# Folding a router into the attention's output projection, with the normalisation applied after the routing choice

## What is computed

```python
x = _layernorm(x + _L1_attn_ref(...))      # ctx (2048 wide: 16 heads x 128) @ w_dense (2048 x 256)
# _L1_ffn_ref, x is 2048 tokens x 256, 8 experts, top 2, capacity 64
logits = x @ router_w.T
probs = softmax(logits); top_p, top_i = top_k(probs, 2)
# first 64 tokens per expert keep their place: buf = rows gathered by (expert, position)
h = gelu(buf @ w1.T + b1) @ w2.T + b2      # then scattered back, times top_p
x = _layernorm(x + out)
```

## Time and profile before

| | |
|---|---|
| median of 3 runs | 897.33 us (894.57 to 899.10) |
| profiled execution | 895.45 us, of which the span of the trace is 893.7 us |
| PE busy | 824.1 us (92% of the span) |
| DVE busy | 693.6 us (78%) |
| ACT busy | 496.5 us (56%) |
| POOL busy | 390.7 us (44%) |
| layer 0 | 0 to about 390 us |
| layer 1's attention, 64 units | about 390 to 816 us |
| last logits and routing | 816 to 830 us |
| gather, expert network, way back | 830 to 894 us |

### The profile page before, as it was taken

One profiled execution on the slowest core, in us unless ns is written; L12 is line 12 of the kernel. 1 busy time (PEld: TensorE's weight loads), 2 busy tenths in 40 slices (PEclk: granted clock), 3 DMA queues, 4 the chain that ended last, 5 costly groups with the idle time before them and its releaser, 6 DMA issues.

```text
span 893.7 us, 22047 instructions
## 1 busy us (share of the span) xinstructions
PE 824.1 (92%) x8209; PEld 512.8 (57%) x8209; DVE 693.6 (78%) x1921; ACT 496.5 (56%) x1181; POOL 390.7 (44%) x731
## 2 busy tenths in 40 slices
PE   6899999997798998979999999999999999997894
PEld 3455555554454544445556766666767766685374
DVE  5777777777688887678999888888888888866535
ACT  3577777765544534456666555656555565532243
POOL 4556576641365664523333333333333333333454
PEclk8999999999899999999999999999999999998998
DMA  5344432420000000016677656556555655550502
GB/s 180 101 120 108 98 73 85 121 32 8 2 1 1 1 1 1 1 30 120 123 117 123 96 104 104 95 103 101 94 100 104 104 104 96 98 91 1 95 1 95
DMA packets 219034, 67.70 MB, mean 76 GB/s; under 512 B 211360, under 2 KB 214704, under 8 KB 218928
## 3 DMA queue, kind: packets, MB, share of 16 engines
q1 hardware_dynamic: 218928, 66.29, 37.8%
HBM read 17.92 MB, written 4.19 MB: 25 GB/s over the span
## 4 chain that ended last, share of the span: by engine, by line
PE 70%; DVE 14%; issue 5%; DMA 4%; ACT 3%; POOL 3%; SPq 1%; POOLq 0%; DVEq 0%; ACTq 0%
PE bank L467 14%; PE bank L469 14%; PE bank L468 14%; PE bank L594 4%; DMA att<-w_lo 4%; PE bank L825 4%; PE bank L827 3%; PE bank L826 3%; DVE nm L1434 3%; PE bank L541 2%; PE bank L536 2%; PE bank L517 2%; DVE w_lo L1458 2%; PE bank L578 1%; DVE scr L1609 1%
## 5 line engine op out<-in xcount | busy, mean ns | idle before, releaser
L1152 ACT ACTIVATE att<-att,nm 128x512 f32<-128x512 f32 (+3 forms) x256 | 141.4, 553 | 104.5 <-DVE nm L1447 103.1
L1057 ACT ACTIVATE scr<-bank 128x512 bf16<-128x512 f32 (+3 forms) x210 | 111.5, 550 | 88.0 <-PE bank L827 46.1
L467 PE MATMUL bank<-w_hi,scr 128*128 128x256 bf16 (+1 forms) x480 | 145.7, 304 | 2.7 <-DVE scr L1376 1.6
L468 PE MATMUL bank<-w_lo,scr 128*128 128x256 bf16 (+1 forms) x480 | 145.4, 303 | 0.0
L469 PE MATMUL bank<-w_hi,scr 128*128 128x256 bf16 (+1 forms) x480 | 145.3, 303 | 0.0
L1434 DVE TENSOR_REDUCE nm<-bank 128x1 f32<-128x512 f32 (+3 forms) x256 | 110.4, 483 | 39.7 <-PE bank L541 39.6
L2065 POOL TENSOR_SCALAR wqkv_hi<-att,rr 128x512 bf16<-128x512 f32 (+3 forms) x128 | 66.1, 536 | 138.7 <-DVE rr L1464 138.7
L1447 DVE CUSTOM_DVE_ANT_0 att<-bank,consts 128x512 f32<-128x512 f32 (+3 forms) x256 | 113.1, 482 | 15.0 <-PE bank L469 15.0
L1103 ACT ACTIVATE att<-bank 128x512 f32<-128x512 f32 (+1 forms) x192 | 90.7, 528 | 50.1 <-PE bank L578 49.7
L1376 DVE TENSOR_TENSOR scr<-bank,scr 128x256 bf16<-128x256 f32 (+1 forms) x146 | 77.3, 539 | 52.5 <-ACT scr L1057 52.1
L2065 POOL TENSOR_SCALAR w_hi<-att,rr 128x512 bf16<-128x512 f32 (+3 forms) x128 | 66.1, 535 | 105.5 <-DVE rr L1464 105.5
(11 more groups left out here) (242 smaller groups left out, 2038.1 us busy)
## 6 DMA issues: line engine op xcount, KB each, us to landing
scr<-wall_in SPq DMA_DIRECT2D x19, 512.0 KB, 4.7
v_by_token<-scr SPq DMA_DIRECT2D x16, 128.0 KB, 1.8
scr<-v_by_token SPq DMA_DIRECT2D x16, 128.0 KB, 3.3
x_tok<-x_tok_in SPq DMA_DIRECT2D x4, 512.0 KB, 5.1
scr<-x_t_in SPq DMA_DIRECT2D x3, 512.0 KB, 5.5
out<-x_tok SPq DMA_DIRECT2D x3, 512.0 KB, 2.6
scr<-wqkv_in SPq DMA_DIRECT2D x2, 384.0 KB, 3.7
att<-w_hi SPq DMA_TRANSPOSE x32, 3.4
```

The lines of the kernel that those rows point to most:

```text
L467: pe.matmul(out, l_hi, r_hi, start=start, stop=False, skip_group_check=check)
L468: pe.matmul(out, l_hi, r_lo, start=False, stop=False, skip_group_check=check)
L1057: return act.activation(out, in_, ACT.Copy)
L1152: last = act.activation(at, at, ACT.Exp, bias=nm[:, j % 2, qt:qt + 1], scale=-1.0, accum_out=rs[:, j % 2, qt:qt + 1])
```

## The change

- The router matrix of layer 1 is centred on the chip (a sum over features by PE, a subtraction by DVE), and multiplied into the 16 heads' blocks of `w_dense`. For that the 16 blocks, high and low, are turned by 32 more DMA transposes (2 blocks of 128x128 each) that SP issues behind `l1_turns(u)`, three in each of u = 1 to 10 and two in u = 11. PE multiplies them in u = 12 to 15 (`fold_router`, 24 matmuls of 8 columns per unit).
- The product is kept as eight more columns beside each head's 256 in `w_hi` and `w_lo`, so that each projection matmul is 264 columns wide. The residual's share of the logits is added by six matmuls of 8 columns per tile. The logits of y thus stand in the same bank as the attention's output.
- `last_turn`, `last_high`, `last_low` and `last_logits` are gone for all 16 tiles.
- Choices are made on logits without r. The exponentials of all tiles come once, in the tail behind the norms of tiles 12 to 15, and are used for the gates alone.
- In the tail, DVE copies the four tiles' logits as each projection ends, then routes. PE adds the residual of tiles 12 to 15 in PSUM with a matmul by the identity (`add_rows`, f32, 256 columns each). DVE takes their statistics between the first `choose` instructions, POOL makes four deviations at once, ACT norms from PSUM. `gather` takes tiles 0 to 11 for both k first, then 12 to 15. The first of two `keep_busy` goes; the iota matmuls come earlier.

The diff, cut:

```diff
+DW = E + NX
+FOLD_FROM, FOLD_LOADS = 12, 32
             for u in range(NH):
                 l1_turns(u)
+                for hd in range(HEADS):
+                    for part, w in enumerate((w_hi, w_lo)):
+                        if (2 * hd + part) // 3 + 1 == u:
+                            sp.dma_start_transpose(wd_t[part][:, KE * hd:KE * (hd + 1), :],
+                                                   w[:, ds(WD + hd * DW, E)]).then_inc(ld_fold, 16)
...
+            def router_mean():
+                pe.wait_ge(eb_ready, 1)
+                for i, part in enumerate((rw_hi, rw_lo)):
+                    for k in range(KE):
+                        last = pe.matmul(bank[7][:, 0:NX], ones_b[:, :], part[:, 1, k * NX:(k + 1) * NX],
+                                         start=(i == 0 and k == 0), stop=(i == 1 and k == KE - 1))
+                last.then_inc(e["mean"], 1)
+
+            def fold_router(heads):
+                pe.wait_ge(e["router"], 1)
+                pe.wait_ge(ld_fold, 16 * FOLD_LOADS)
+                for hd in heads:
+                    for k in range(KE):
+                        ks = slice(k * NX, (k + 1) * NX)
+                        last = mm3(bank[7][:, hd * NX:(hd + 1) * NX], wd_t[0][:, hd * KE + k, :], wd_t[1][:, hd * KE + k, :],
+                                   router_hi[:, ks], router_lo[:, ks], k == 0, k == KE - 1, True)
...
-                    ws = slice(WD + hd * E, WD + (hd + 1) * E)
-                    last = mm3(out, ct_hi[:, cs], ct_lo[:, cs], w_hi[:, ws], w_lo[:, ws], hd == 0, hd == HEADS - 1)
+                    ws = slice(WD + hd * DW, WD + (hd + 1) * DW)
+                    last = mm3(out, ct_hi[:, cs], ct_lo[:, cs], w_hi[:, ws], w_lo[:, ws], hd == 0, hd == HEADS - 1, True)
+                    if hd == 0:
+                        for k in range(KE):
+                            xs, ks = ds((g - TT) * P, P), slice(k * NX, (k + 1) * NX)
+                            mm3(out[:, E:DW], xt_hi[:, k, xs], xt_lo[:, k, xs], router_hi[:, ks], router_lo[:, ks],
+                                False, False, True)
...
+            def add_rows(t):
+                pe.matmul(bank[DENSE_BANKS[t % TT]][:, 0:E], ident_f, x_tok[:, t * E:(t + 1) * E], start=False, stop=True,
+                          skip_group_check=True).then_inc(e["sum"], 1)
...
-                    if g > TT and j == 2:
-                        hold(pe, c["kvl"], 2 * min(g + 1, NT - 1) + 2)
-                        last_turn(g - TT - 1)
-                    if g > TT and j == 3:
-                        last_logits(g - TT - 1)
+                    if u == TT:
+                        router_mean()
+                    if FOLD_FROM <= u < 4 * TT:
+                        first = 4 * (u - FOLD_FROM)
+                        fold_router(range(first, first + 4))
...
             pe.wait_ge(c["max"], 3 * NH)
+            iota_rows()
...
-            last_turn(DONE)
-            last_turn(DONE + 1)
-            last_logits(DONE)
...
-            pe.wait_ge(e["lgc"], DONE + 1)
-            keep_busy(FILL)
+            pe.wait_ge(e["lgc"], NT)
+            for t in range(DONE, NT):
+                add_rows(t)
             ranks()
             keep_busy(FILL)
             for k in range(KE):
-                for t in range(NT):
+                for t in range(DONE):
+                    gather(k, t)
+            for k in range(KE):
+                for t in range(DONE, NT):
                     gather(k, t)
...
             act.wait_ge(e["cnt"], 1)
             copy(count_b, bank[5][:, 0:2 * P]).then_inc(e["cntb"], 1)
+            act.wait_ge(c["rstd"], DONE + 1)
+            for t in range(DONE, NT):
+                act.activation(x_tok[:, t * E:(t + 1) * E], bank[DENSE_BANKS[t % TT]][:, 0:E], ACT.Identity,
+                               bias=shift_t[:, t:t + 1], scale=rstd_x[:, t:t + 1]).then_inc(e["xn"], 1)
+            act.wait_ge(e["xn"], TT)
+            copy(row_hi[:, DONE * E:NT * E], x_tok[:, DONE * E:NT * E]).then_inc(e["rhi"], 1)
+            act.wait_ge(e["scaled"], 1)
+            act.activation(powers, scaled, ACT.Exp).then_inc(e["ex"], 1)
...
+            for t in range(DONE, NT):
+                dve.wait_ge(c["o"], t + 1)
+                dve.tensor_copy(lg[:, t, :], bank[DENSE_BANKS[t % TT]][:, E:DW]).then_inc(e["lgc"], 1)
+            dve.wait_ge(e["lgc"], NT)
             route_tiles(DONE, NT, 2)
...
-            for t in range(2 * TT):
+            for t in range(DONE):
+                choose(t)
+                if t in (3, 4, 5, 6):
+                    deviation(DONE + t - 3)
+            for t in range(DONE, NT):
                 choose(t)
             rows = slice(DONE * E, NT * E)
             dve.wait_ge(e["rhi"], NB)
             low(row_lo[:, rows], x_tok[:, rows], row_hi[:, rows]).then_inc(e["rlo"], 1)
-            for t in range(2 * TT, NT):
-                choose(t)
```

More of the change, by code:

```diff
@@ L207, in build, with dense_rows, chunk_at, staged @@
         iota8 = consts[:, 768:768 + P]
+        def dense_rows(w):
+            return w[:, WD:WD + HEADS * DW].rearrange("p (h c) -> p h c", c=DW)
+        def chunk_at(w, n):
+            if n in DENSE_CHUNKS:
+                first = 4 * (n - DENSE_CHUNKS[0])
+                return dense_rows(w)[:, first:first + 4, 0:E]
+            return w[:, ds(n * CH + (HEADS * NX if n > DENSE_CHUNKS[-1] else 0), CH)]
+        def staged(n):
+            part = stage[:, ds((n % 2) * CH, CH)]
+            return part.rearrange("p (h c) -> p h c", c=E) if n in DENSE_CHUNKS else part
+        spare = past[:, :, :].rearrange("p i c -> p (i c)").bitcast(F32)
+        router_f, rstd_x = spare[:, 0:KE * NX], spare[:, 32:32 + NT]
+        router_hi, router_lo = [spare[:, 16 + 8 * i:24 + 8 * i].bitcast(BF16) for i in range(2)]
+        wd_t = [scr[:, 4096 + 2048 * i:6144 + 2048 * i].bitcast(BF16).rearrange("p (b q) -> p b q", q=P) for i in range(2)]
         qt_hi = [w_hi[:, TOK * i:TOK * (i + 1)] for i in range(2)]
@@ L334, in build @@
         e = {n: sem(f"ffn_{n}") for n in (
-            "tp", "thi", "tlo", "lg", "lgc", "lgd", "ex", "picks", "rank", "gates", "h", "ge", "hhi", "hlo",
+            "lgc", "ex", "mean", "router", "fold", "fhi", "folded", "sum", "xn", "scaled", "picks", "rank", "gates", "h", "ge", "hhi", "hlo",
             "y", "yr", "bg", "xb", "seq", "agg", "rstd", "x", "dve", "iota", "iotad", "rhi", "rlo", "pick",
@@ L828, in l1_pv @@
                 last.then_inc(c["pv"], 1)
+            def router_mean():
[13 more added lines that the diff above has]
+                                   router_hi[:, ks], router_lo[:, ks], k == 0, k == KE - 1, True)
+                if heads[-1] == HEADS - 1:
+                    last.then_inc(e["fold"], 1)
             def dense_heads(out, g, heads):
@@ L1702, in l1_norm, with center_router, folded_low @@
                 rows = x_tok[:, ds(t * E, E)]
-                i = max(0, t - DONE)
                 hold(dve, c["rstd"], t + 1)
-                dve.tensor_scalar(rows, rows, mv[:, i, 0:1], rstd[:, i:i + 1], ALU.subtract, ALU.mult
+                dve.tensor_scalar(rows, rows, mv[:, 0, 0:1], rstd_x[:, t:t + 1], ALU.subtract, ALU.mult
                                   ).then_inc(c["x"], 1)
+            def center_router():
+                dve.wait_ge(e["mean"], 1)
+                chain = Chain(dve, e["dve"], 0)
+                for k in range(KE):
+                    ks = slice(k * NX, (k + 1) * NX)
+                    chain(dve.scalar_tensor_tensor(router_f[:, ks], bank[7][:, 0:NX], -1.0 / E, rw_f[:, 1, ks],
+                                                   ALU.mult, ALU.add))
+                chain(dve.tensor_copy(router_hi[:, :], router_f[:, :]))
+                dve.tensor_tensor(router_lo[:, :], router_f[:, :], router_hi[:, :], ALU.subtract).then_inc(e["router"], 1)
+            def folded_low():
+                dve.wait_ge(e["fhi"], 1)
+                low(dense_rows(w_lo)[:, :, E:DW], bank[7][:, 0:HEADS * NX].rearrange("p (h c) -> p h c", c=NX),
+                    dense_rows(w_hi)[:, :, E:DW]).then_inc(e["folded"], 1)
             def l1_group(g, dense):
@@ L1777, in route_tiles @@
                 chain(dve.tensor_tensor(first[:, ts, :], rev[:, ts, :], wide(2), ALU.is_equal))
-                dve.wait_ge(e["ex"], turn)
-                chain(dve.scalar_tensor_tensor(row(3), first[:, ts, :], -2.0, row(1), ALU.mult, ALU.add))
+                chain(dve.scalar_tensor_tensor(row(3), first[:, ts, :], FAR, row(0), ALU.mult, ALU.add))
                 chain(dve.tensor_reduce(r1c[:, 1, ts], row(3), AX.X, ALU.max))
@@ L2080, in _ @@
                 rows_low(b)
-            for t in range(DONE, NT):
-                inverse_deviation(t % TT, c["mv"], t + 1, c["seq"], t + 1, c["rstd"])
+            inverse_deviation(DONE, TT)
             def gated_bias(t):
```

180 lines of the change are left out of this document (66 added, 114 removed).

## The result

The changed kernel takes 915.39 us in the median of six runs (914.07 to 917.93), beside 897.64 us (894.22 to 899.10) for the kernel before: ratio 1.020, 95% interval 1.0179 to 1.022. It is 2.0% slower, 12 us above the upper end of the predicted range.

The account below looks back on a forecast made before the run. PE was taken to bound layer 1's attention, with a 7.9 us hole in the tail to win. Terms +2.9 + 1.0 + 2.9 - 6.7 = +0.1 gave 896.5 us, range 890 to 903.5 for 8 in 10.

Parts of the forecast that it names:

- Three more transposes per unit: SP's queue, units 1 to 11: small transposes issue in 0.83 us each, low ones land late; +1.0 us in sum.
- the bound of +11: Upper bound for the added transposes' crowding over 11 units, where +1.0 us was taken and 0 was the lower bound.
- Two of my own signs of being wrong: Prediction wrong if, among others, a small issue is over 1.1 us or the fold's idle under 2 or over 4.5.
- SP becomes the bound: Rival, chance 0.12: small transposes issue in 1.33 us, SP needs 6.7 us per unit of 6.0; sum about +10, 906.
- The fold's wait: Unit 12: PE waits 3.5 us for the last turned blocks, bounds 2.3 and 4.4; -0.6 won back, net +2.9.
- The wait also costs the clock: Rival, chance 0.16: unit 12's wait lowers the granted clock, +1.5, with crowding +3; sum +5, 901.5 us.
- PE's own work: PE to the end of the projections: tiles 0 to 11 -0.8, tiles 12 to 15 +1.2, fold +2.4, mean +0.1; +2.9.
- The tail: Behind the last projection: routing starts 7.6 us earlier, inserted deviations give back 0.9; -6.7 us, bounds -7.6 and -4.

Follow-up runs that it names:

- probe: The kernel with all 32 small transposes ahead of unit 0, plus 21 transposes of 1 to 32 blocks, each waited for, in SP's empty stretch; one execution 894.17 us.
- late_fold: Against the changed kernel, the fold's matmuls moved from units 12 to 15 to units 14 to 17, copies in unit 17; 911.25 us, ratio 1.0152.
- early: Against the changed kernel, all 32 small transposes issued ahead of unit 0, where SP's queue is empty; 892.52 us, ratio to the kernel before 0.9953.
- tail_pairs: Transposes ahead of unit 0, and in the tail both gathers of tiles 0 to 11 in one turn, deviations behind the first four choices; 892.42 us, ratio 0.994.

## Why the prediction was wrong, point by point

**Three more transposes per unit** is the step that failed, three times over. The term was +1.0 us; the stretch measured +16.9 against +1.1. First the price: 0.83 us came from a line through 10 and 16 blocks, prolonged to 2. Measured 1.25, close to my own upper bound of 1.33; the probe shows that the line bends at about 8 to 10 blocks. Of two bounds 0.33 and 1.33, the second was from the same instruction on the same queue, the nearer row. Second the period: I set 5.2 us of SP against the 6.0 us of the stretch 448 to 472, while the mean from high(1) to high(12) was 5.44 (even in the stretch that I read, high(10) to high(14), 450.88 to 473.44, it was 5.64). Third, a packed queue costs more than the sum of lone issues: the low transpose directly behind a high one takes 1.52 where it took 1.33, and 0.04 to 0.1 us lie between any two. For three small ones to fit, an issue would have to be under (5.44 - 1.35 - 1.52 - 0.25) / 3 = 0.77 us. Even my 0.83 would have filled the queue. I had also taken a high transpose that comes late as harmless by itself; what SP has free ahead of the next high one is about 1.6 us in the kernel before, room for one small transpose and not for three. Crowding came out at +16.9, and the bound of +11 that I gave was too low by the same mistakes. A little of it may be the clock's: from 402 to 424 us the granted clock was 0.92 in the kernel after and 1.00 before. Two of my own signs of being wrong came: an issue over 1.1 us (1.25) and an idle of the fold over 4.5 (5.62).

**The rival *SP becomes the bound*** (0.12) is what happened. Its mechanism was right, its size was half: "6.7 us per unit of 6.0" was 7.1 of 5.44 (403.41 to 481.51 for high(1) to high(12), 78.1 / 11), and 11 x 1.66 = 18 is near the 16.9 measured, where it said 7. Its argument against, "the issue grew between 10 and 16 blocks", looked at the slope and not at the constant. The Trainium skill (DMA: Bandwidth & Descriptors, "Rules for kernel authors") says to coalesce many small transfers, and that under 64 KB one pays mostly overhead; a small transpose here moves 64 KB, just at that figure. The runs agree with the first half: eight transposes of eight blocks took 894.69 us, 32 of two 915.39. I took the rule for the issue's price alone, when it spoke about the count. The Trainium skill (DMA: Bandwidth & Descriptors, "Issuing engines are not separate DMA queues") calls the sequencer's time to start a DMA usually small relative to the DMA; here it is not small, 1.25 of the 2.4 us to the landing.

**The fold's wait**: 5.62 us of idle, not 3.5. The landing was placed well: predicted 463.7 - 458.64 = 5.1 us behind the start of low(11), measured 482.71 - 477.22 = 5.5. But PE stood there 1.6 us behind that start before, and now 0.1 us ahead of it (477.09), since everything but SP had time to spare. A wait's length is the difference of two times, and I had moved only one.

***The wait also costs the clock*** (0.16) happened too: granted clock 0.55 in the 6 us behind the wait. Together the wait and the clock cost 4.7 us of the stretch in `late_fold`'s comparison, against +2.9 and, with the clock, some +4.4. The clock alone wasn't measured apart from the wait. In the rows of PE the matmuls from 483.35 to 487.36 go at half pace, so it holds back some 2 us of PE work, an estimate from these starts.

**PE's own work** held, as far as the traces can tell. Without crowding, high(0) to low(63) is +0.7 us in `early`, and +0.0 to +2.2 over the four traces with that code, where the terms up to there give +1.7 (fold 2.4, mean 0.1, tiles 0 to 11 -0.8). From low(63) to the end of the projections the kernel after took 18.9 us against 18.4 (822.40 to 841.33, 797.62 to 816.02): +0.5, where I had +1.2. Matmuls of 264 columns start 0.112 us apart in the mean, those of 256 columns in the kernel before 0.109: the 0.003 that I had worked out, so a head's block every 264 columns costs nothing.

**The tail** held in sum. The first `choose` came 7.8 us earlier behind the projections (7.6 predicted), the stretch to the copy behind the last gather grew by 1.0 (16.4 us, where I had 16.2 behind the first `choose`, S). Two sizes were off, unseen in the sum, and that they stayed unseen is partly luck: the four f32 `add_rows` took 1.99 us, over both my figures, under routing's cover; POOL's power on four columns took 1.48 us against the 0.55 of one column that I had set as its upper bound. The chain behind it, low half at 857.94, was at S + 10.9 to S + 12.1, just in time against my 12.8: PE did not idle before the last gathers.

The sum with measured terms: +16.9 + 4.6 + 1.6 - 6.2 = +16.9 from high(0) on, beside +1.7 in layer 0, of which no run shows that it is the change's. The medians of the runs differ by 17.8.

## What to carry to other kernels

Price each added DMA by its issue first, count issues and not bytes (here up to 8 blocks an issue), and take the price from the smallest transfer of the same kind in the trace as a constant, not from a line prolonged below it. Take the period from the distance of like starts. A queue with room on average can still have too little at the place where the new work stands: here one small transpose fitted ahead of the next high one, two did not, and what they delay is whatever stands behind in the same order. So work needed only later belongs in a stretch where the queue is empty, as here in layer 0. When one actor is made later, recompute when the others arrive before sizing a wait.

## What the runs showed that was not expected

- A transpose of 1 to 8 blocks of 128x128 costs SP the same, 1.12 to 1.25 us mostly, one of 10 blocks 1.33, of 16 blocks 1.75, of 32 blocks 4.8.
- Some issues take 0.6 to 1 us longer without anything in the trace to explain it (2.29 at 430.61; 1.76 of 1.20 in the probe). The cause stays open.
- POOL's power instruction grows with its columns: 0.55 us for 128x1, 1.48 us for 128x4, which is about 0.3 us per further column, an estimate from these two sizes. Doing four at once saved less than it seems.
- Layer 1 starts up to 6 us apart (397.3 to 403.1) between traces of kernels whose layer 0 is nearly the same. The granted clock goes with it in part: from 200 to 240 us it was 1.00 in the kernel before (397.3) and 0.91 in `tail_pairs` (403.1), but 1.00 as well in `probe` (402.1). The rest of the cause stays open.
